# Attention and slot-mixture kernel: gathering the slots already transposed, with the dispatch softmax divided on ScalarE, and new instruction orders on every engine

## The reference

```python
# layer 1, on a layer-normalised x
q = exp(heads(x @ Wq.T + bq)); k = exp(heads(x @ Wk.T + bk)); v = heads(x @ Wv.T + bv)
kv = cumsum(k[:, :, :, None] * v[:, :, None, :], axis=1)
out = einsum('zsD,zsDd->zsd', q, kv) / sum(q * cumsum(k, axis=1), -1)
x = x + layernorm(out @ Wo.T + bo)
# layer 2, on a layer-normalised x
xn = rms_norm(x, gamma_x); se = rms_norm(slot_embeds, gamma_slot)
logits = einsum('bsd,etd->bset', xn, se)
dispatch = softmax(logits, axis=1)            # over the 256 tokens, for each slot
slots = einsum('bsd,bset->betd', xn, dispatch)
h = gelu(slots @ w1); processed = h @ w2      # 128 -> 512 -> 128
combine = softmax(logits over the 512 slots)  # for each token
x = x + layernorm(einsum('bnd,bsn->bsd', processed, combine))
```

## Time and profile before

| | |
|---|---|
| median of 3 runs | 631.2 us (631.08 to 632.29) |
| profiled execution | 632.58 us, span 630.9 us, mean granted TensorE clock 0.992 |
| PE busy | 598.0 us (95%), 4294 instructions |
| DVE busy | 474.5 us (75%), 922 instructions |
| ACT busy | 438.5 us (70%), 1087 instructions |
| POOL busy | 483.4 us (77%), 495 instructions |

### The profile page before, as it was taken

The page is one execution under the profiler, slowest core; times in us unless marked ns, Lnnn a source line. Parts: engine busy times, 40 slices in busy tenths (PEclk is TensorE's granted clock), DMA queues, the critical chain, the costliest instruction groups (busy, mean ns, idle before and its releaser), DMA issues.

```text
span 630.9 us, 12020 instructions
## 1 busy us (share of the span) xinstructions
PE 598.0 (95%) x4294; PEld 531.8 (84%) x4294; DVE 474.5 (75%) x922; ACT 438.5 (70%) x1087; POOL 483.4 (77%) x495
## 2 busy tenths in 40 slices
PE   7876999999999999999999999999999999999886
PEld 6765888888989888889898888888988888888875
DVE  6988578887777788887777878877777888767521
ACT  4234777777777777777777777777777777777745
POOL 5989687888888888888888888888888888873100
PEclk9898999999999999999999999999999999999999
DMA  3000000000000000000000000000000000000000
GB/s 107 11 19 17 18 26 18 22 13 27 26 25 26 26 18 27 10 26 26 26 26 26 17 26 10 26 26 26 26 26 19 25 14 22 18 18 9 9 10 17
DMA packets 16831, 14.36 MB, mean 23 GB/s; under 512 B 2851, under 2 KB 16645, under 8 KB 16773
## 3 DMA queue, kind: packets, MB, share of 16 engines
q1 hardware_dynamic: 14708, 12.76, 6.7%
q10 hardware_dynamic: 2064, 0.86, 0.5%
HBM read 5.25 MB, written 4.19 MB: 15 GB/s over the span
## 4 chain that ended last, share of the span: by engine, by line
PE 51%; DVE 23%; ACT 17%; POOL 3%; issue 3%; DMA 2%; SPq 0%; DVEq 0%; POOLq 0%; ACTq 0%
PE HB L917 16%; DVE WB L1185 12%; PE LA L894 9%; ACT L477 6%; PE LA L873 5%; ACT comb L597 5%; PE WB L845 3%; PE WB L755 2%; ACT slT_hi L474 2%; PE LB L883 2%; DVE xnT_lo L1142 2%; DVE att L1195 2%; PE WB L796 2%; PE WB L829 2%; ACT xnT_hi L474 2%
## 5 line engine op out<-in xcount | busy, mean ns | idle before, releaser
L917 PE MATMUL HB<-w_c,hid 128*128 128x128 f32 x992 | 120.8, 275 | 0.5 <-ACT hid L481 0.5
L917 PEld LDWEIGHTS HB<-w_c,hid 128*128 128x128 f32 x992 | 117.3, 192 | 0.7 <-ACT hid L481 0.7
L481 ACT ACTIVATE hid<-HB 128x512 f32<-128x512 f32 x128 | 76.7, 599 | 32.9 <-PE HB L757 27.2
L214 POOL TENSOR_TENSOR kv<-E 128x1024 f32<-128x1024 f32 x32 | 68.4, 2136 | 33.8 <-ACT E L474 33.7
L1170 DVE TENSOR_TENSOR prod<-WB,E 128x768 f32<-128x768 f32 x96 | 91.0, 949 | 3.6 <-PE WB L846 3.6
L1185 DVE TENSOR_REDUCE WB<-prod 128x288 f32<-128x2304 f32 x32 | 82.0, 2562 | 3.1
L338 POOL TENSOR_TENSOR kv_lo<-kv,kv_hi 128x1152 fp32r<-128x1152 f32 x31 | 82.4, 2658 | 2.5
L398 POOL TENSOR_TENSOR kv<-kv,kv_prev 128x1024 f32<-128x1024 f32 x31 | 74.1, 2391 | 0.0
L214 POOL TENSOR_TENSOR kv_prev<-prev 128x1024 f32<-128x1024 f32 x31 | 66.4, 2141 | 5.2 <-DMA prev<-E 5.2
L930 PE MATMUL LA<-proc,comb 128*128 128x129 f32 x512 | 62.5, 274 | 1.5 <-ACT proc L474 1.5
L894 PE MATMUL LA<-xn,disp 128*128 128x129 f32 x512 | 62.6, 275 | 0.5 <-ACT disp L474 0.4
(11 more groups left out here) (145 smaller groups left out, 1548.9 us busy)
## 6 DMA issues: line engine op xcount, KB each, us to landing
X<-in_L_attn_x_dram SPq DMA_DIRECT2D x32, 128.0 KB, 2.1
out_dram<-res SPq DMA_DIRECT2D x32, 128.0 KB, 1.8
prev<-E SPq DMA_DIRECT2D x32, 112.0 KB, 2.1
w_in<-in_L_ffn_w_dram ACTq DMA_DIRECT2D x2, 256.0 KB, 4.6
prev<-E SPq DMA_DIRECT2D x32, 15.0 KB, 2.0
se_in<-n_L_ffn_slot_embeds_dram ACTq DMA_DIRECT2D x1, 256.0 KB, 3.7
w_in<-in_L_attn_Wq_dram SPq DMA_DIRECT2D x1, 64.0 KB, 2.4
w_in<-in_L_attn_Wk_dram SPq DMA_DIRECT2D x1, 64.0 KB, 2.2
```

The source lines that it names most:

```text
L214: return eng.tensor_tensor(dst.rearrange("p (d h e) -> p d h e", d=HD, h=NH), k.rearrange("p (o h e) -> p o h e", o=1, h=NH).broadcast_to( ...
L481: act.activation(hid[:, f, :], HB[:, f % 2, :], ACT.Gelu).then_inc(gelu_ready[f], 1)
L917: last = pe.matmul(PR[:, j, :], hid[:, f, j * P:(j + 1) * P], w2_c[:, f, :], start=(f == 0), stop=(f == FJ - 1))
```

## The change

The dispatch softmax is divided before the gather. `dispatch_exp` also accumulates its sum (`disp_sum`), a new `dispatch_inverse` on DVE takes the reciprocal, and a new `dispatch_scale` on ACT multiplies `disp_t` in place, in four instructions of 256 columns. `gather_slots` swaps its operands: `xn` is stationary and `disp` moves, 512 columns at a time, so the slots come out transposed, straight into `HB[:, 0, :]`. `slots_scale`, `slots_transpose`, the tile `slots` and the column of ones in `xn` go.

All the programs are written in new orders, and waits that another wait covers are left out. In the steady step the second half of `process` moves on PE from behind `dispatch_transpose` to ahead of `cumulate(.., 0)`, and `x_transpose` goes between the halves of `hidden`. On DVE `x_statistics` moves ahead of `attention`. On ACT the values are copied before the exponentials of `q` and `k`, and the exp table is loaded at a place of its own. The prologue has more `spin` matmuls (141 of them instead of 79), SP shifts `prev` of batch 2 ahead of the load of batch 4, and the epilogue loses `process_last` (the last batch's `process` interleaved with `hidden`) and the split of its mixture.

```diff
+            def dispatch_exp(n):
+                act.wait_ge(max_ready, n + 1)
+                for j in range(SJ):
+                    last = act.activation(disp_t[:, j, :], LBv[:, j, :], ACT.Exp, bias=neg_max[:, j:j + 1], accum_out=disp_sum[:, j:j + 1])
+                last.then_inc(disp_exp, 1)
...
+            def dispatch_scale(n):
+                act.wait_ge(disp_inverted, n + 1)
+                for j in range(SJ):
+                    last = act.activation(disp_t[:, j, :], disp_t[:, j, :], ACT.Copy, scale=disp_inv[:, j:j + 1])
+                last.then_inc(disp_scaled, 1)
...
+            def gather_slots(n):
+                pe.wait_ge(disp_ready[0], n + 1)
+                for c in range(NC):
+                    last = pe.matmul(HB[:, 0, :], xn[n % 2][:, c, :], disp[:, c, :], start=(c == 0), stop=(c == NC - 1))
+                last.then_inc(slT_done, 1)
...
+            def dispatch_inverse(n):
+                dve.wait_ge(disp_exp, n + 1)
+                dve.reciprocal(disp_inv[:, :], disp_sum[:, :]).then_inc(disp_inverted, 1)
...
-            def slots_scale(n):
-                after(dve, slots_done, n)
-                dve.reciprocal(disp_inv[:, :].rearrange("p (g j) -> p g j", g=2), SL[:, :, :, DIM]).then_inc(slots_inv, 1)
-                after(dve, slots_inv, n)
-                dve.tensor_tensor(slots[:, :, :].rearrange("p (g j) d -> p g j d", g=2), SL[:, :, :, 0:DIM],
```

More of the change, by code:

```diff
@@ L217, in outer, with each_batch, run @@
                 v.rearrange("p (h d o) -> p d h o", d=HD, o=1).broadcast_to((P, HD, NH, HD)), ALU.mult)
[L219 to L227, removed]
+        def each_batch(op):
+            def run(n, *tile):
+                if 0 <= n < NB:
+                    op(n, *tile)
+            return run
         block = ctx.enter_context(nc.Block())
@@ L471, in _ @@
+            first_steps()
+            for s in range(6, 38):
+                step(s)
         @block.scalar
@@ L586, in dispatch_exp @@
                 last.then_inc(disp_exp, 1)
[L588 to L598 removed]
+            @each_batch
@@ new lines, in first_steps @@
+                hidden(1, 0)
+                hidden(1, 1)
+                x_transpose(5)
+                hidden(1, 2)
+                hidden(1, 3)
+                logits(2)
+                att_transpose(3)
+                project(5, 0)
+                project(5, 1)
+                process(1, 0)
+                attention_out(3)
+                part_transpose(2)
+                process(1, 1)
+                cumulate(4, 0)
+                dispatch_transpose(2, 1)
+                dispatch_transpose(2, 0)
@@ new lines, in first_steps, with step @@
+                cumulate(4, 1)
+                subtract_max(2)
+                cumulate(4, 2)
+                gather_slots(2)
+                xn_transpose(3)
+                mixture(1)
+                hidden(2, 0)
+                hidden(2, 1)
+            def step(s):
+                x_transpose(s)
+                hidden(s - 4, 2)
+                hidden(s - 4, 3)
+                logits(s - 3)
+                att_transpose(s - 2)
+                project(s, 0)
+                project(s, 1)
+                process(s - 4, 0)
+                attention_out(s - 2)
+                part_transpose(s - 3)
+                process(s - 4, 1)
+                cumulate(s - 1, 0)
+                dispatch_transpose(s - 3, 1)
+                dispatch_transpose(s - 3, 0)
+                subtract_max(s - 3)
+                cumulate(s - 1, 1)
+                cumulate(s - 1, 2)
+                gather_slots(s - 3)
+                xn_transpose(s - 2)
+                mixture(s - 4)
+                hidden(s - 3, 0)
+                hidden(s - 3, 1)
@@ L1056, in _ @@
+            first_steps()
+            for s in range(6, 32):
+                step(s)
+            last_steps()
         @block.vector
@@ L1320, in first_steps @@
+                own_sum(1)
+                multiply(1, 2)
                 xnT_low(0)
-                attention(1, 1)
+                attention_sums(1)
+                x_statistics(4)
+                attention(1)
                 xT_low(3)
```

1332 lines of the change are left out of this document (665 added, 667 removed).

## The result

| | before | after |
|---|---|---|
| median | 631.97 us (16 runs, 631.0 to 632.69) | 635.86 us (16 runs, 632.82 to 640.1) |
| ratio | | 1.0067, 95% interval 1.0049 to 1.0085 |
| profiled span | 630.9 us | 634.6 us |
| mean granted TensorE clock | 0.992 | 0.996 |

The kernel became slower by 0.7%, where 3% faster was predicted, and its runs scatter over 7 us where those of before scatter over 1.7.

What follows compares the result with a forecast made beforehand. PE was taken as the bound, with short waits for the DVE and ACT loop. 28 periods falling from 18.0 to 17.3 gave 632.6 - 19.6 - 0.7 (last period) + 1.3 (epilogue) = 613.6, median 612 us; range 602 to 627.

Steps and rivals of the forecast that it cites:

- Where they come to lie: Steady step, timed from the `att` transposes: when ACT, DVE and PE pieces start and end, summing to a 17.3 us period.
- PE now stalls 0.4 there: PE ahead of the first `cumulate`: it waits 0.4 us for `tok_max`, where it had waited 0.22.
- PE's own work: PE's work per steady step without waits: 17.97 less 0.49 of slot transposes and 0.73 of idle, 16.75 us.
- under the logits: ACT's exp table load of 1.28 us, ahead of the `attT` copy, was placed during PE's logits matmuls.
- The scaled copies: Four 256-column copies of `disp_t` on ACT each step: about 1.7 us, bounds 1.28 and 2.9.
- The reads of the sums: Accumulated sums on ACT's dispatch exponentials: about 0.1 us each, 0.4 for four, between nothing and 1.0.
- The rest of the epilogue: After the last period: about 1 us lost net, 3 at most; entered in the sum as 1.3 lost.
- A: The forecast itself: PE stays the bound with ties, period around 17.3 (17.1 to 17.5), 607 to 618 us; chance 0.58.
- B: Ties lost through slower copies, reads or a DVE piece caught by POOL: period 17.6 to 17.85, 618 to 629; chance 0.22.
- C: The 0.4 stall is absent, ACT and DVE starting earlier: period 16.9, prologue wins 3 us, 598 to 607; chance 0.10.
- E: Slower: DVE's `xn` or `xh` meets a long POOL product on the shared port, 1.8 late; period 19.1, 662 us; chance 0.07.
- a sign of failure: In each steady step, a wait of over 0.5 us for the scale or for `disp` would show the prediction wrong.

Runs made afterwards that it cites:

- the first experiment: The kernel after with one edit in SP's step: the store of a result is issued ahead of the shift of `prev`; 613.57 us, ratio 0.9711.
- both experiments without the wait: The kernel after with the store ahead of the shift (613.57 us), and the kernel after with four `res` buffers and store semaphores instead of two (613.26 us).
- the arithmetic alone: The kernel before with the new sums, reciprocal, scaled copies and transposed gather, all other orders, waits and idle matmuls as before; 709.74 us, ratio 1.1233.

## Why the prediction was wrong

**The step that failed** is "Where they come to lie", in the sentence on DVE: "two pieces of 0.60 each, overlapping to about 0.5, and then `tok_max`, 0.42: it is ready at 6.3". The stall that it led to, "PE now stalls 0.4 there", measured 1.39 in the kernel after. The sentence takes `res` to be ready to run once `xh` is out of the way. `second_residual` also waits for the store of batch n - 2, and where that store is issued is decided in SP's step, which the diff reordered and the prediction never opened. It names PE, DVE and ACT as the timelines read; of SP it speaks only in the prologue. The chance of "slower" was put on another mechanism.

The numbers for it stood in the trace of before. The dispatch exponentials were put at 2.6, and those of `E` just ahead of them end about 0.1 later, at 2.7; the two shifts of before take 1.44, and its page has a median of 1.8 from the issue of a store to its landing. That gives 2.7 + 1.44 + 1.8 = 5.9 for `res`, and with 0.5 and 0.42 for `tok_max` 6.9, where 7.27 was measured (308.70 - 301.43) and 6.3 predicted. `cumulate` would have started at 7.0 instead of 6.28, and the period would have been 17.3 + 0.7 = 18.0, that of before; it is 18.11.

Point by point, each time counted from the transposes of `att`, predicted, then measured in the kernel after, then in the first experiment's:

| | predicted | after | store first |
|---|---|---|---|
| first exponential | 2.6 | 2.70 | 2.69 |
| reciprocal ends | 4.85 | 4.85 | 4.85 |
| scale | 4.95 to 6.65 | 5.00 to 6.74 | 4.99 to 6.74 |
| `tok_max` ready | 6.3 | 7.27 | 6.19 |
| first `cumulate` starts | 6.28 | 7.42 | 6.33 |
| transposes of `disp_t` | 6.8 | 7.84 | 6.79 |
| gather starts | 8.96 | 9.89 | 9.02 |
| period | 17.3 | 18.11 | 17.34 |

But for the store each of these times holds to 0.11 us, and with the store in time so does the sum: 612 predicted, 613.6 measured. That the sum is so near is partly luck, since two terms of the period miss and cancel. PE's own work was put at 16.75, and the kernel after leaves 18.11 - 1.39 - 0.37 = 16.35. The 0.37 is PE's wait for ACT's copy of `attT` (302.00 to 302.55, less 0.18 for the instruction); the prediction had put the table load ahead of that copy "under the logits", at nothing. A small reading is wrong as well: 0.21 for a 512-column fp32r instruction does not follow from the gather's columns, which would give 0.42; the hidden matmuls of before are issued every 0.23, so the gap there is 0.17 and not 0.19.

The scaled copies took 1.74 for the predicted 1.7. The Trainium skill, "ScalarE: Activation LUTs", says in the section on what ACT_TABLE_LOAD costs also that ACTIVATEs back to back overlap by some 93 ns, which the prediction left out; by estimate from that page four copies then take 1.69 and not 1.97, and the trace agrees. The reads of the sums stretched the exponentials from 1.42 to 1.80, by the predicted 0.4. ACT's busy time rose by 57 us, not by 70 to 85; the group of the scaled copies alone is 55.6, and where ACT got the time of the reads back was not traced.

**The sum.** From batch 2 to batch 30 the kernel after needs 574.37 - 65.34 = 509.0 us, where 28 x 17.3 = 484.4 were predicted: this difference of 24.6 is all of the miss (635.9 against 612). The first three of these steps still have 17.34 to 17.42. The next is the one in which `res` of batch 2 is made, the first that has to wait for a store, and from there on it is 18.0 to 18.1. Four longer steps (21.15, 18.93, 18.55 and 18.44) add 4.7. In the longest `res` waits 2.46 for its store and in the others 1.82, 1.43 and 1.35, where the usual wait is 1.0: in these three the excess is the whole of it. In the prologue nothing was predicted with 4 us either way, and it won 0.5 (65.34 against 65.89). The last period won 0.9 for the predicted 0.7. The rest of the epilogue, predicted at 1.3 lost, lost nothing in the kernel after and 1.5 with the store first (45.4 against 43.9). These 1.5 are the clock. Behind the same wait of 2.66 us for `disp_t` of the last batch the granted clock read 0.58 with the store first and 1.00 in the kernel after; their last gathers, in this order:

```profile
593.43 3.40 PE L895 MATMUL HB<-disp,xn 128*128 128x512 f32 x4 [0.17 <-ACT disp L453]
...
616.20 1.98 PE L895 MATMUL HB<-disp,xn 128*128 128x512 f32 x4 [0.27 <-ACT disp L453]
```

**The rivals.** A, B and C each have PE or its ties as the bound; the steady step without the late store has the period of A. E was right in form (something makes DVE late, with `tok_max` behind it, and it decides from 0.7 of delay a step on: the period is 0.77 over that without the store's wait) and wrong in its mechanism: no `xh` or `xn` meets a long product in the steady step, they last 0.57 and 0.59. The experiment with the late store in the old orders shows that this was luck of the order and not a rule: there the late store brings `xh` and the product together. But it shows too that the meeting need not cost anything: PE lost the wait for the store and no more. What the prediction had named as a sign of failure, a wait of over 0.5 for the scale or `disp`, did not appear either; the sign was a DMA as releaser in DVE's rows.

**Not settled.** Which of the small waits would have to go together to get below 17.3 was not tried beyond single edits. That the jitter of the stores, and the clock that sometimes falls behind it, spread the runs over 7 us is read from one profiled execution, from the scatter of 2 us in both experiments without the wait, and from the mean granted clock (1.000 in the fastest run, 0.993 in the slowest); the landings in the other executions were not seen.

## What to carry to other kernels

When a change rewrites all the orders, write down for every engine's step what each wait is released by, SP's queue included: an instruction of 0.6 us that writes a buffer waits for the transfer that reads it, and that transfer waits for whatever stands ahead of it in its queue. In a queue, put what is ready ahead of what waits; the store here, whose data had long been ready, cost nothing ahead of the shift and 0.8 us a step behind it. The Trainium skill, "DMA: Bandwidth & Descriptors", rules for kernel authors, has for the overlap of a transfer with compute the rule to issue it early and to wait for it late; the first experiment agrees with it. And when single edits of a tuned loop each win nothing, look at whether the waits are tied before more of them are tried: here those for `tok_max`, the scale and `xn` stood in for one another to 0.05 us.

## What the runs showed of the hardware

A wait of PE of over 2 us can have a second price, and doesn't always. Where the granted clock fell behind one, it read 0.54 to 0.60 in windows of 2 to 4 us, and the fall cost 1.4 to 1.6 us beyond the wait: a step of 22.0 instead of 20.5 (the late store in the old orders), 21.2 instead of 19.6 (the arithmetic alone), 1.4 in the last gather above. In the kernel after it fell once in the steady part, behind a wait that the profile puts at 2.61; windows of that step:

```profile
197.00:200.00 3.00, 1.36 (x11) 1.36 (x11) 2.20 (x6) 0.90 (x5) 1.58 (x1) 0.97 0.00 0
200.00:204.00 4.00, 4.00 (x13) 3.00 (x13) 2.48 (x6) 2.14 (x4) 1.90 (x5) 0.59 0.11 33
204.00:210.90 6.90, 6.90 (x46) 5.95 (x45) 5.79 (x12) 5.96 (x13) 5.68 (x5) 1.00 0.00 1
```

The waits of the other steps of that run, 1.12 to 1.98 by the same measure, didn't bring it down. But neither did every longer one. Of 27 equal waits of 2.12 in the arithmetic alone it fell behind 14; of the 22 of 2.44 to 2.49 with the late store in the old orders it fell behind 5, and behind all three of 2.83 to 3.44; behind 2.66 in the epilogue it fell in one profiled execution and not in another. What decides between two like waits, no run here shows. For a plan it is enough that a wait of over 2 us in a loop is a bet on another 1.5.

In the prologue without idle matmuls the granted clock reads 1.00 throughout, and yet the matmul behind a wait of 4.46 us takes 0.66 where it takes 0.42, and those behind it are issued every 0.32 us where they are issued every 0.18. Another run of the same kernel has a mean granted clock of 0.955 and the same time (616.53 against 616.34 at 0.999). So that column does not show every slow stretch; the lengths do.

A store of 128 KB landed in 1.7 to 3.9 us over the kernels before and after, with the same median of 1.8 to 1.9. Such a spread is hidden while nobody waits, and a late one is paid when the landing is on the path.
